# Expert stage of a linear-attention and mixture-of-experts layer: more PSUM banks and buffers, and another order of the down projection

## The reference

```python
probs = jax.nn.softmax(jnp.einsum('bsd,ed->bse', x, choice_w), axis=-1)
G, I = jax.lax.top_k(jnp.swapaxes(probs, -1, -2), k)            # k = 1024 rows for each expert and batch
x_in = jnp.take_along_axis(x[:, None, :, :], I[..., None], axis=2)
h = jax.nn.silu(jnp.einsum('bekd,edf->bekf', x_in, w1))         # 512 -> 1024
x_mlp = jnp.einsum('bekf,efd->bekd', h, w2)                     # 1024 -> 512
out = jnp.zeros_like(x).at[b_idx, I].add(G[..., None] * x_mlp)
```

## Time and profile before

| | |
|---|---|
| time, median of 3 runs (lowest to highest) | 2497.65 us (2490.52 to 2500.5) |
| the profiled execution: its own time | 2497.8 us |
| its span, first to last instruction | 2495.9 us |
| PE busy | 2396.7 us, 96% of the span |
| DVE, ACT, POOL busy | 54%, 33%, 43% |
| expert stage, first to last large matmul | 943.96 to 2486.67 us |

### The profile page before, as it was taken

The page is one execution under the profiler, slowest core; times in us unless marked ns, Lnnn a source line. Parts: engine busy times, 40 slices in busy tenths (PEclk is TensorE's granted clock), DMA queues, the critical chain, the costliest instruction groups (busy, mean ns, idle before and its releaser), DMA issues.

```text
span 2495.9 us, 34661 instructions
## 1 busy us (share of the span) xinstructions
PE 2396.7 (96%) x12544; PEld 2013.4 (81%) x12544; DVE 1345.1 (54%) x2654; ACT 831.3 (33%) x1458; POOL 1077.1 (43%) x959
## 2 busy tenths in 40 slices
PE   8999999999999999999998998999999998999898
PEld 7889988898999887777776786787786787787677
DVE  7777776687777786334335245245245245245331
ACT  4445544454454553122223223223223223223111
POOL 0100034200002565565665565566565565566441
PEclk9999999999999999999999999999999999999999
DMA  7555334355544446224224223324324323322122
GB/s 198 160 126 142 105 58 73 56 152 151 129 123 80 60 79 142 44 41 113 49 43 107 49 48 81 69 50 108 54 48 94 58 51 77 73 49 45 35 39 30
DMA packets 125947, 205.38 MB, mean 82 GB/s; under 512 B 28264, under 2 KB 53480, under 8 KB 125552
## 3 DMA queue, kind: packets, MB, share of 16 engines
q0 software_dynamic: 57088, 118.02, 26.5%
q1 hardware_dynamic: 68720, 85.42, 11.6%
HBM read 119.22 MB, written 100.93 MB: 88 GB/s over the span
## 4 chain that ended last, share of the span: by engine, by line
PE 89%; issue 4%; DVE 4%; another core or an unknown queue 1%; ACT 1%; DMA 1%; POOL 0%; POOLq 0%; DVEq 0%; SPq 0%; ACTq 0%
PE ps L1351 29%; PE ps L1353 28%; PE ps L1352 28%; PE ps L1444 2%; PE ps L1581 1%; DVE h_lo L1318 1%; PE ps L1378 1%; DVE one_lo L906 1%; DVE h_hi L1316 0%; DMA xo<-in_L_attn_x_dram 0%; DMA normed_rows<-xo 0%; DVE w_lo L1322 0%; DVE stats L810 0%; DVE qT L1034 0%
## 5 line engine op out<-in xcount | busy, mean ns | idle before, releaser
L462 POOL DMA_INDIRECT rows<-normed_rows,idx_row x512 | 540.1, 1055 | 156.1 <-issue 156.1
L1351 PE MATMUL ps<-w_hi,h_hi 128*128 128x512 f32 x1024 | 414.2, 404 | 43.4 <-issue 29.9
L570 POOL DMA_INDIRECT out_dram<-y,idx x128 | 227.9, 1780 | 477.1 <-ACT y L792 473.7
L1351 PE MATMUL ps<-xi_hi,w_hi 128*128 128x512 f32 x1024 | 406.7, 397 | 8.7 <-issue 8.6
L1352 PE MATMUL ps<-w_lo,h_hi 128*128 128x512 f32 x1024 | 408.3, 399 | 5.3 <-issue 5.2
L1353 PE MATMUL ps<-w_hi,h_lo 128*128 128x512 f32 x1024 | 407.9, 398 | 2.8 <-issue 2.6
L1316 DVE CAST h_hi<-hf 128x512 fp32r<-128x512 f32 x256 | 111.2, 435 | 546.5 <-issue 289.8
L1352 PE MATMUL ps<-xi_lo,w_hi 128*128 128x512 f32 x1024 | 401.9, 392 | 0.0
L1353 PE MATMUL ps<-xi_hi,w_lo 128*128 128x512 f32 x1024 | 400.3, 391 | 0.8 <-issue 0.7
L772 ACT ACTIVATE hf<-ps 128x512 f32<-128x512 f32 x256 | 153.0, 598 | 666.3 <-PE ps L1353 448.2
L1351 PEld LDWEIGHTS ps<-w_hi,h_hi 128*128 128x128 f32 x1024 | 198.1, 193 | 92.4 <-issue 42.4
(11 more groups left out here) (176 smaller groups left out, 4117.9 us busy)
## 6 DMA issues: line engine op xcount, KB each, us to landing
xo<-in_L_attn_x_dram SPq DMA_DIRECT2D x32, 512.0 KB, 4.7
normed_rows<-xo SPq DMA_DIRECT2D x32, 512.0 KB, 4.5
out_dram<-bo POOLq DMA_DIRECT2D x16, 1024.0 KB, 9.1
out_dram<-xo POOLq DMA_DIRECT2D x64, 256.0 KB, 4.0
w_raw<-in_L_ffn_w_dram SPq DMA_DIRECT2D x32, 512.0 KB
w_raw<-in_L_ffn_w_dram SPq DMA_DIRECT2D x8, 2048.0 KB
xn<-normed_rows SPq DMA_DIRECT2D x96, 128.0 KB, 2.4
rows<-normed_rows,idx_row POOLq DMA_INDIRECT x512
```

What stands on the lines that cost most here:

```text
L462: nc.gpsimd.indirect_dma_start(rows[:, tt, a, :], None, pieces[:, :], bass.IndirectOffsetOnAxis(ap=idx_row[:, b, tile, a:a + 1], axis=0)). ...
L570: nc.gpsimd.indirect_dma_start(of[:, :], bass.IndirectOffsetOnAxis(ap=idx[:, u * TPB + tt:u * TPB + tt + 1], axis=0), y[:, tt, :], None, c ...
L1351: nc.tensor.matmul(dst, a_hi, b_hi, start=start, stop=False, skip_group_check=True)
```

## The change

- Up projection: three banks in turn (0, 1, 7) in place of two. PE waits before part m for the silu of part m - 3. In the first unit's part 2 it also waits for `rank_out`.
- `hf` has four buffers in place of two. The silu of part m waits for the split of part m - 4.
- Down projection: each of the four parts has a bank of its own (2, 3, 5, 6). PE waits once, before the first, for all of the previous unit's y. The order is: k = 0 to 5 of tt 0, of tt 1 and of tt 3; then k = 6, 7 of tt 0 and of tt 1; then all of tt 2; then k = 6, 7 of tt 3. The waits for `h_ready` stay with tt 0. `spread` comes after the first piece of tt 1, `list_rows` after DVE's tt = 2 step.
- `y` has two sets of four tiles (unit u writes set u % 2), and ACT waits for the adds of the unit before the last. It now does all four `rows_hi` (and in the last unit of an expert all eight `w1_high`) before its first wait for a down part.

```diff
+LATE = KF - 2
+UP_BANKS, DOWN_BANKS = (0, 1, 7), (2, 3, 5, 6)
+HF, YS = 4, 2
...
-            hf = sb("hf", [P, 2, BLK])
-            y = sb("y", [P, TPB, D])
+            hf = sb("hf", [P, HF, BLK])
...
+            y = sb("y", [P, YS, TPB, D])
...
                     for m in range(KF):
                         act.wait_ge(up_done, n * KF + m + 1)
-                        act.wait_ge(h_ready, AHEAD + n * KF + max(m - 1, 0))
-                        nc.scalar.activation(hf[:, m % 2, :], ps[:, m % 2, :], ACT.Silu).then_inc(silu_done, 1)
+                        act.wait_ge(h_ready, AHEAD + n * KF + max(m - HF + 1, 0))
+                        nc.scalar.activation(hf[:, m % HF, :], ps[:, UP_BANKS[m % 3], :], ACT.Silu).then_inc(silu_done, 1)
...
-                    if u == 0 and e > 0:
-                        act.wait_ge(added[B - 1], e * (16 * SLOT_TILES))
-                    elif u > 0:
-                        before = u - 1
-                        act.wait_ge(added[before // HALVES],
-                                    (e * SLOT_TILES + (before % HALVES + 1) * TPB) * 16)
                     for tt in range(TPB):
                         if n + 1 < E * UNITS:
                             rows_hi(n + 1, tt)
-                        act.wait_ge(down_done, AHEAD + n * TPB + tt + 1)
-                        if tt == 0:
-                            act.wait_ge(gain_in[u % 2], e * (64 * UNITS // 2) + (u // 2 + 1) * 64)
-                        apart(act)
-                        nc.scalar.activation(y[:, tt, :], ps[:, 2 + tt % 2, :], ACT.Copy,
-                                             scale=gain[:, u % 2, tt, bass.ds(e, 1)]).then_inc(y_ready, 1)
                         if u == UNITS - 1 and e < E - 1:
                             if tt == 0:
                                 act.wait_ge(w1_in, (e + 2) * (HPG * 16))
                             for m in (2 * tt, 2 * tt + 1):
                                 w1_high(m)
+                    if n >= YS:
+                        before = n - YS
+                        act.wait_ge(added[before % UNITS // HALVES],
+                                    (before // UNITS * SLOT_TILES + (before % HALVES + 1) * TPB) * 16)
+                    elif n > 0:
+                        for s in range(RES):
+                            act.wait_ge(out_stored[s], 16 * B * NT // RES)
+                    for tt in range(TPB):
+                        act.wait_ge(down_done, AHEAD + n * TPB + tt + 1)
+                        if tt == 0:
+                            act.wait_ge(gain_in[u % 2], e * (64 * UNITS // 2) + (u // 2 + 1) * 64)
+                        apart(act)
+                        nc.scalar.activation(y[:, u % YS, tt, :], ps[:, DOWN_BANKS[tt], :], ACT.Copy,
+                                             scale=gain[:, u % 2, tt, bass.ds(e, 1)]).then_inc(y_ready, 1)
...
-                        if made and tt == 1:
+                        if made and tt == 2:
                             list_rows(of_b, turn)
...
-                        pe.wait_ge(silu_done, AHEAD + n * KF + max(m - 1, 0))
+                        pe.wait_ge(silu_done, AHEAD + n * KF + max(m - 2, 0))
+                        if u == 0 and m == 2:
+                            pe.wait_ge(rank_out, B)
                         for k in range(KD):
-                            last = product(ps[:, m % 2, :], pair(w1s, al, k, slice(m * P, (m + 1) * P)),
+                            last = product(ps[:, UP_BANKS[m % 3], :], pair(w1s, al, k, slice(m * P, (m + 1) * P)),
                                            pair(xi, al, k, al), k == 0, k == KD - 1)
...
-                    for tt in range(TPB):
-                        pe.wait_ge(y_ready, AHEAD + n * TPB + max(tt - 1, 0))
-                        for k in range(KF):
+                    pe.wait_ge(y_ready, AHEAD + n * TPB)
+                    if u == 0:
+                        pe.wait_ge(fin, AHEAD + B * NT)
+                    parts = [(0, 0, LATE), (1, 0, LATE), (3, 0, LATE), (0, LATE, KF), (1, LATE, KF), (2, 0, KF), (3, LATE, KF)]
+                    for tt, k_from, k_to in parts:
+                        for k in range(k_from, k_to):
                             if tt == 0:
                                 pe.wait_ge(h_ready, AHEAD + n * KF + (k + 1))
                                 if u == 0:
                                     pe.wait_ge(w2_ready, e * KF + (k + 1))
-                            last = product(ps[:, 2 + tt % 2, :], pair(hs, al, k, slice(tt * P, (tt + 1) * P)),
+                            last = product(ps[:, DOWN_BANKS[tt], :], pair(hs, al, k, slice(tt * P, (tt + 1) * P)),
                                            pair(w2s, al, k, al), k == 0, k == KF - 1)
-                        last.then_inc(down_done, 1)
-                        if u % HALVES == 0 and tt == 0:
+                        if k_to == KF:
+                            last.then_inc(down_done, 1)
+                        if u % HALVES == 0 and tt == 1 and k_from == 0:
                             spread(e * B + (u // HALVES + 1))
```

More of the change, by code:

```diff
@@ L571, in expert @@
                             of[:, :], bass.IndirectOffsetOnAxis(ap=idx[:, u * TPB + tt:u * TPB + tt + 1], axis=0),
-                            y[:, tt, :], None, compute_op=ALU.add).then_inc(added[b], 16)
+                            y[:, u % YS, tt, :], None, compute_op=ALU.add).then_inc(added[b], 16)
             with pool.Fori(0, E - 1) as e:
@@ L1315, in _ @@
                             dve.wait_ge(down_done, AHEAD + n * TPB)
-                        me.did(nc.vector.tensor_copy(h_hi[:, m, :], hf[:, m % 2, :]))
+                        me.did(nc.vector.tensor_copy(h_hi[:, m, :], hf[:, m % HF, :]))
                         me.wait()
-                        nc.vector.tensor_tensor(h_lo[:, m, :], hf[:, m % 2, :], h_hi[:, m, :].bitcast(F32),
+                        nc.vector.tensor_tensor(h_lo[:, m, :], hf[:, m % HF, :], h_hi[:, m, :].bitcast(F32),
                                                 ALU.subtract).then_inc(h_ready, 1)
```

## The result

The changed kernel takes 2592.39 us (median of four runs, 2583.55 to 2597.68) against 2499.07 for the kernel before beside it: a ratio of 1.0342 (95% interval [1.0302, 1.0381]). The prediction was 2419.

The account below looks back on a forecast made before the run. PE, busy for 96% of the span, was taken to bound the kernel. From 2497.8 us, less 51 (down order) and 28 (up banks and hf), plus 0.5 (tail), came 2419.3; the 8 in 10 range was 2385 to 2462.

Parts of the forecast that it names:

- Floors and the 122 us: Expert stage, PE: odd down, even up and even down phases exceed their undisturbed times by 122 us, the most to win.
- I take the late signals to be something that the gathers bring.: PE's signals to ACT: about 5.9 us late in unit 9, taken to come from POOL's gathers, without knowing how.
- The new down order, -51: Odd down phases: h of part 7 needed later, so its pauses and half clock go; 51 us gained, 8 left.
- rival 5: PE's pause in unit 9 is its own, the missing silu coincides; nothing changes, 2490 to 2505 us; chance 0.06.
- POOL's adds bunch: POOL, end of down phases: last add and next gather start about 1 us later, hidden within the unit.
- Three up banks and four hf, -28: Even up phases: silus may come some 3 us later, so pauses in six units go; 28 us gained.
- What moves and what it costs: Moved waits and ACT's earlier rows_hi and w1_high: priced at no cost apart from 0.5 us at the end.
- The tail, +0.5: Very end of the stage: the last add starts 1.7 us after the last matmul, before 1.2; cost 0.5 us.
- 35 of the stage's 256 silus were released in this late way: ACT, expert stage: count of silus that started after an idle time ended by "remote", read as late PE signals.
- Rival 2: Late signals get worse; pauses at list matmuls and first k of down phases; gains 40 and 0, 2458 us; chance 0.18.
- Rival 3: Signal leaves only when PE runs dry; PE stops at k = 6 in units with a gather; 2568 us; chance 0.04.
- Rival 4: Seven banks in turn make PE's stream ragged: one more half-clock stretch per unit, 1.1 us each; 2454 us; chance 0.03.

Follow-up runs that it names:

- e5: e3 with GpSimd waiting after each tile's four row gathers until they have landed; 2391.43 us, ratio 0.9545.
- e6: e3 with each gather after the first fetching only one of a row's four pieces, without waits for landing; 2385.88 us, ratio 0.9518.
- e17: Kernel before the change with only the gather paced by fours, in the session with the most pauses; 2379.94 us against 2596.96, ratio 0.9174.
- e3: Changed kernel, but SyncE loads the next expert's w1 only after the second silu of the expert's first unit; 2531.17 us, ratio 1.0066.
- e8: e3 with the down parts in the old order, tiles 0 to 3 done whole; 2522.26 us, ratio 1.0047.
- e7: e3 with only tiles 0 and 1 split at k = 6 in the down order, tiles 2 and 3 done whole; 2491.64 us, ratio 0.9915.
- e1: Kernel before the change with only the three up banks, four hf buffers and the wait for rank_out; 2510.23 us, ratio 1.0024.
- e13: The changed kernel, unedited, in a session where the kernel before shows no losses (2378.9 us); 2420.73 us, ratio 1.0174.
- e16: e3 with sixteen row gathers of 32 rows each in place of 128, not paced, in a session without losses; 2385.5 us, ratio 1.0027.
- e11: e3 with the gather paced after every eight row gathers, in a session without losses; 2384.81 us, ratio 1.0027.
- e2: Changed kernel with two up banks and two hf buffers again; 2588.72 us, ratio 1.0215, runs scattered from 2548 to 2601.
- e19: The same kernel as e16, in a session with pauses; 2664.78 us against 2518.05, ratio 1.0587.
- e15: Changed kernel with the early w1 load kept and the gather paced by fours, in a session without losses; 2407.49 us, ratio 1.01.

## Why the prediction was wrong

- *Floors and the 122 us.* Right: with pacing every phase is at these floors, and 2497.8 - 122 = 2376 is within 4 us of what the kernel before takes when its gather is paced or its session has no pauses.
- *"I take the late signals to be something that the gathers bring."* Right, by e5, e6 and e17.
- *The new down order, -51.* Its first half is right: the pause at the 22nd matmul is gone from all odd units. The step that failed is "what may stay in odd units are pauses in which PE waited for nothing shown ... I leave 8 us". I took these pauses at the size that they had behind the wait for h, and took them to stay at it. With the wait gone they grew, at the same place, from 0.7 to 1.1 us to 1.4 to 2.8, and the odd down phases are 66 us over their floor in e3, where I left 8. That is nearest to rival 5 ("then the pause comes wherever PE is at that time"), to which I gave 0.06. Its sign was in the rows: the small pauses came behind the short waits and not behind the long ones. The term is 31 us at best (e8 to e7).
- *POOL's adds bunch, "so this hides".* Also priced at nothing. The order of the change, in which they bunch, costs 38 us against that of e7. That the bunching is the cause was argued, not shown.
- *Three up banks and four hf, -28.* Wrong: 0 (e1, within half a per cent of 2507). The same mistake: behind the wait that I took away was a pause that no wait explained, and it stayed.
- *"What moves and what it costs ... nothing."* The costliest step. I priced `w1_high` before y at ACT and DVE ("ends sooner than before") and did not ask whom the earlier end releases. It is SyncE's 2 MB load, which moved from the up phase into the last down phase, beside PE's loop branch, which needs a DMA of its own. It costs 35 us where nothing else disturbs (e13 against e16, 2420.7 to 2385.5; e11, with whole rows paced by eights, took 2384.8). It costs about 69, with less certainty (58 or 37 against e2), where the gather disturbs PE too, part of it then in the up phase that follows: u = 0 lost 45 us. Why that phase suffers by more than the 12 us of e13 is open.
- *The tail, +0.5.* The stage's end to the span's end went from 9.3 to 9.8 us: right.
- *"35 of the stage's 256 silus were released in this late way".* That row counts only those whose release has no sender in the profile. By their times of start it was 48.
- *Rival 2* had the sign of the even up phases (over 24 us on average: 28.7), not the size. *Rival 3*, the slower one, named a mechanism that isn't there: no pause at the 55th matmul of any down phase; that its 2568 is nearest to the time is chance. *Rival 4*: the odd up phases, which now use three banks in turn, are at 348.15, so changes of bank cost nothing here. The Trainium skill's page TensorE: Matmul & The Clock Gate, section A second HAM failure mode: psum-queue depth-cycling, describes a kernel in which they did; by these rows this is not one.
- *Semaphores.* The Trainium skill's page Advanced Engine Details and Errata, section DMA Bandwidth Details, puts the overhead of an increment at about one cycle. The trace agrees in sessions without pauses, where every silu starts 0.2 to 0.4 us after its part's last matmul (e13), and not in the others (up to 15.3 us in the changed kernel). The page speaks of the increment alone; which step between PE and ACT is late there, no row tells.

So the 173 us between 2419.3 and 2592.4 are 78.5 of gain that did not come and 94.6 of loss, counted from 2497.8. The result is made up like this, in ratios to the kernel before in sessions with pauses: banks, buffers and ACT's order with the old down order and the late load 1.0047 (e8), h of parts 6 and 7 needed later 0.9915 (e7), the change's own order 1.0066 (e3), the early w1 load 1.0342 (the changed kernel). These come from three sessions, so each step carries their difference as well.

What stays open: what differs between sessions, since one chip gave 2379 and 2518 for the same kernel. And by what path POOL's rows of indirect transfers hold PE up; whether a wait is needed to break them, or POOL issuing more slowly would do, wasn't tried either. All times here are of executions with records taken; whether that plays a part wasn't tried.

## What to carry to other kernels

When the bottleneck engine waits for a late signal, look at whether it could have gone on at all. Small pauses without a wait, close behind the waits, are a sign that it could not: here they grew when the waits went, and both went only when POOL's gather was broken up. When a producer is moved earlier, follow its semaphore to every queue that waits on it, the DMA queues above all, and ask what their transfers now lie beside. Long rows of indirect transfers are worth breaking up with a wait for their landing: four at a time cost nothing here, and took off up to 8%. Do not let a large load start in the last microseconds before a loop's branch.

## What of the hardware I had not expected

- Some twenty indirect DMAs issued back to back by POOL (1.3 us apart) went with signals of PE that took effect up to 12.5 us late (15.3 in the changed kernel) and with stops of PE's matmuls for 2 us and more; with 2.3 us of idle POOL after each four (e5, e17), neither is left.
- Whether this happens is a property of the session: the same kernel took 2385.5 (e16) and 2664.8 us (e19) on one chip.
- PE's loop branch takes 3.3 to 3.9 us in the kernel before, hidden by matmuls given earlier, and 6.2 to 9.3 when a 2 MB load was issued ahead of it, of which up to 4.7 shows in e13 and 5.6 in e15. It ends 1.1 to 1.6 us after a transfer of 16 KB of code has landed, and the load holds that transfer back.
